# Adding three parts by accumulation on TensorE and one key subtraction on GpSimd, in the adjacency stage of a graph network

## The reference, cut to what matters

```
def _gcn_conv(x, src, dst, W, b, num_nodes):
    h = x @ W
    loops = jnp.arange(num_nodes, dtype=src.dtype)
    s = jnp.concatenate([src, loops])
    d = jnp.concatenate([dst, loops])
    deg = jax.ops.segment_sum(jnp.ones_like(d, dtype=h.dtype), d, num_segments=num_nodes)
    dinv = jnp.where(deg > 0, jax.lax.rsqrt(deg), 0.0)
    norm = dinv[s] * dinv[d]
    msg = h[s] * norm[:, None]
    out = jax.ops.segment_sum(msg, d, num_segments=num_nodes)
    return out + b
```

## Time and profile before

| | us |
|---|---|
| median of 3 runs | 10569.1 (10568.56 to 10575.79) |
| the profiled execution, its own time | 10570.14 |
| its span, first to last instruction | 10568.4 |
| outside the span in that execution | 1.7 |
| first pass, steady part looked at | 2262 to 2885 |
| second pass, steady part looked at | 2960 to 3250 |

### The profile page before, as it was taken

The page is one execution under the profiler, slowest core; times in us unless marked ns, Lnnn a source line. Parts: engine busy times, 40 slices in busy tenths (PEclk is TensorE's granted clock), DMA queues, the critical chain, the costliest instruction groups (busy, mean ns, idle before and its releaser), DMA issues.

```text
span 10568.4 us, 124127 instructions
## 1 busy us (share of the span) xinstructions
PE 5527.7 (52%) x33901; PEld 4454.6 (42%) x33999; DVE 6613.1 (63%) x9196; ACT 2250.9 (21%) x3204; POOL 7100.7 (67%) x7048
## 2 busy tenths in 40 slices
PE   4666656459886666666644423333333434333333
PEld 3444444348885555445522213333333333333333
DVE  6777777789913555555578855555555555555555
ACT  1111111148700111111158821111111111111111
POOL 6777777626604777777755537777777577777774
PEclk8777787679997888888855555556556655556566
DMA  8777777524486777777756625555555355555552
GB/s 182 195 196 194 196 197 197 149 91 206 194 341 219 233 236 237 240 233 234 238 185 203 203 64 125 124 125 124 126 124 126 74 126 124 126 123 126 125 126 67
DMA packets 2347310, 1784.10 MB, mean 169 GB/s; under 512 B 1805829, under 2 KB 1977610, under 8 KB 2342282
## 3 DMA queue, kind: packets, MB, share of 16 engines
q1 hardware_dynamic: 774743, 879.12, 25.3%
q10 hardware_dynamic: 1356944, 617.91, 21.4%
q0 software_dynamic: 215456, 284.72, 11.7%
HBM read 921.34 MB, written 861.11 MB: 169 GB/s over the span
## 4 chain that ended last, share of the span: by engine, by line
POOL 53%; issue 22%; DVE 12%; PE 5%; ACT 4%; DMA 2%; ACTq 1%; SPq 1%; POOLq 0%; DVEq 0%
POOL arena L601 52%; DVE obuf L1894 3%; ACT arena L1116 2%; POOL feat L693 2%; PE ph L927 2%; PE pn L927 1%; DVE neg L1894 1%; DVE pos L1894 1%; ACT obuf L1086 1%; DMA arena<-in_x_dram,idx_src 1%; ACTq L1089 1%; ACT arena L1122 1%; DVE work L1437 0%; DVE arena L1476 0%; PE pn L763 0%
## 5 line engine op out<-in xcount | busy, mean ns | idle before, releaser
L601 POOL DMA_INDIRECT arena<-table_d,idx_src x3136 | 2959.0, 944 | 1123.4 <-issue 955.4
L765 PE MATMUL pn<-work,wblk 128*128 128x128 f32 x3136 | 1049.9, 438 | 2386.3 <-DMA arena<-table_d,idx_src 2386.3
L765 PEld LDWEIGHTS pn<-work,wblk 128*128 128x128 f32 x3136 | 838.0, 327 | 2525.6 <-issue 1844.9
L601 POOL DMA_INDIRECT arena<-in_x_dram,idx_src x1568 | 1495.7, 954 | 514.5 <-issue 469.4
L601 POOL DMA_INDIRECT arena<-tsrc_d,idx_src x1568 | 1479.5, 944 | 477.9 <-issue 477.9
L1378 DVE TENSOR_SCALAR idx_src<-src_all 128x8 int32 (+1 forms) x784 | 147.9, 190 | 2317.9 <-PE pn L766 1590.1
L766 PE MATMUL pn<-ident,arena 128*128 128x128 f32 x4704 | 1375.3, 392 | 0.0
L766 PEld LDWEIGHTS pn<-ident,arena 128*128 128x128 f32 x4704 | 1177.1, 306 | 0.0
L1476 DVE STREAM_TRANSPOSE arena<-work 128x512 f32<-128x512 f32 x1568 | 991.4, 680 | 98.2 <-DVE work L1437 98.2
L1437 DVE TENSOR_TENSOR_SCAN work<-keep,work,pn 128x512 f32<-128x512 bf16 x588 | 752.8, 1280 | 245.4 <-PE ph L778 200.9
L755 PE MATMUL pn<-work,weT 128*128 128x512 f32 x784 | 552.0, 794 | 663.3 <-DMA arena<-tsrc_d,idx_src 634.0
(11 more groups left out here) (402 smaller groups left out, 11166.3 us busy)
## 6 DMA issues: line engine op xcount, KB each, us to landing
runs_d<-arena ACTq DMA_DIRECT2D x2352, 192.0 KB
adj_d<-feat SPq DMA_DIRECT2D x37, 3136.0 KB, 10.8
seed_d<-nothing SPq DMA_DIRECT2D x392, 256.0 KB
arena<-seed_d SPq DMA_DIRECT2D x392, 256.0 KB, 6.8
attr<-in_edge_attr_dram SPq DMA_DIRECT2D x392, 256.0 KB
feat<-total_d SPq DMA_DIRECT2D x196, 512.0 KB
keep<-keep_d SPq DMA_DIRECT2D x588, 128.0 KB
feat<-adj_d SPq DMA_DIRECT2D x37, 1600.0 KB, 9.0
```

What stands on the lines that cost most here:

```text
L601: g.indirect_dma_start(out=to, out_offset=None, in_=table, in_offset=bass.IndirectOffsetOnAxis(ap=idx, axis=0))\
L765: mm(to, wblk[:, PNA.index(p), j, :], feat_to[u], start=True, stop=False, skip_group_check=True)
```

## The change

Two things move. `sum_parts` goes: `local_sum` on PE now multiplies the selection with each of the three parts in turn, reading `vraw` where `vsum` was, and lets the three products accumulate in PSUM. `sums_out` on ACT, which refills `vraw`, therefore waits for PE's product and not for DVE's addition. And `keys` moves from DVE to POOL: it stands there behind the gather of the next step and ahead of the scatter.

```
-                mm(pe_[:, 1, 0:P], pick[:, m % 4, :], vsum[:, m, :], start=True, stop=True,
-                   skip_group_check=True).then_inc(s_used, 1)
+                for k in range(3):
+                    last = mm(pe_[:, 1, 0:P], pick[:, m % 4, :], vraw[:, m % 2, :, k, :], start=(k == 0), stop=(k == 2),
+                              skip_group_check=True)
+                last.then_inc(s_used, 1)
...
-                pe.wait_ge(s_vs, 2 * (MT * x + m + 1))
+                pe.wait_ge(s_vc, MT * x + m + 1)
...
-                    act.wait_ge(s_vs, 2 * (n - 1))
+                    act.wait_ge(s_used, 2 + (MT + 1) * x + m - 1)
...
+                    if m:
+                        keys(m - 1)
                     if m >= ROWS_LAG:
                         local_rows(0, m - ROWS_LAG)
+                keys(MT - 1)
+
+            def keys(m):
+
+                if m == 0:
+                    g.wait_ge(s_kl, 4)
+                g.wait_ge(s_near[m % 2], 16 * (m // 2 + 1))
+                g.sem_inc(s_in_order, 1)
+                g.tensor_scalar(near[:, m % 2, :, 0], near[:, m % 2, :, 0], key0[:, m:m + 1], None, ALU.add).then_inc(s_key, 1)
...
-            def keys(m):
-
-                dve.wait_ge(s_near[m % 2], 16 * (m // 2 + 1))
-                TS(near[:, m % 2, :, 0], near[:, m % 2, :, 0], key0[:, m:m + 1], None, ALU.add).then_inc(s_key, 1)
...
-            def sum_parts(x, m, k):
-
-                n, to = MT * x + m, vsum[:, m, :].rearrange("p (j c) -> p j c", j=2)
-                if k == 0:
-                    dve.wait_ge(s_vc, n + 1)
-                    TT(to, vraw[:, m % 2, :, 0, :], vraw[:, m % 2, :, 1, :], ALU.add).then_inc(s_vs, 1)
-                else:
-                    dve.wait_ge(s_vs, 2 * n + 1)
-                    TT(to, to, vraw[:, m % 2, :, 2, :], ALU.add).then_inc(s_vs, 1)
...
-                            if n == 2 and m + 1 < MT:
-                                keys(m + 1)
-                            if n in (4, 5) and m >= 2:
-                                sum_parts(0, m - 2, n - 4)
```

More of the change, by code:

```diff
@@ L174, in gnn_kernel @@
         key_w = [a[:, :, :].rearrange("p s n -> p (s n)")[:, 0:HOT * KC].rearrange("p (n c) -> p n c", c=KC) for a in (neg, pos)]
-        vsum = work[:, 0:MT * 2 * F].rearrange("p (m n) -> p m n", m=MT)
         rest = work[:, 0:NT * F].rearrange("p (w c) -> p w c", c=F)
@@ L279, in gnn_kernel @@
             "s_tb", "s_td", "s_tail", "s_mi", "s_mid", "s_sc"))
-        s_nat, s_kl, s_key, s_nT, s_nC, s_hts, s_bd, s_ev, s_ap, s_vc, s_vs = (sem(n) for n in (
-            "s_nat", "s_kl", "s_key", "s_nT", "s_nC", "s_hts", "s_bd", "s_ev", "s_ap", "s_vc", "s_vs"))
+        s_nat, s_kl, s_key, s_nT, s_nC, s_hts, s_bd, s_ev, s_ap, s_vc = (sem(n) for n in (
+            "s_nat", "s_kl", "s_key", "s_nT", "s_nC", "s_hts", "s_bd", "s_ev", "s_ap", "s_vc"))
         s_pick, s_used, s_cc, s_ag = (sem(n) for n in ("s_pick", "s_used", "s_cc", "s_ag"))
@@ L1952, in neighbour_sums @@
                     split_table()
-                    keys(0)
                     run_tables()
@@ L1965, in neighbour_sums @@
                     for m in (MT - 2, MT - 1):
-                        sum_parts(0, m, 0)
-                        sum_parts(0, m, 1)
                         pick_run(0, m)
@@ L1971, in neighbour_sums @@
                     for m in range(MT):
-                        sum_parts(1, m, 0)
-                        sum_parts(1, m, 1)
                         pick_run(1, m)
```

## The result

| | us |
|---|---|
| median of 6 runs after | 10649.72 (10646.02 to 10670.37) |
| median of 6 runs before | 10569.65 (10568.56 to 10577.38) |
| ratio | 1.0078 (1.0065 to 1.0090) |
| profiled execution after, its own time | 10670.37 |

A forecast was written before the change was run, and what follows sets the result against it. DVE was taken to bound the first pass, PE the second. 0.2 - 21.2 + 5.4 + 0.8 + 17.0 + 0.9 = +3.1 us on 10570.14, median 1.0 lower: 10572.2, range 10560 to 10588 (own case 10563 to 10581).

The forecast's parts named there:

- The keys on POOL: First pass: keys on POOL stretch DVE's two-input operations by 0.15 us each, 36 x 0.15 = 5.4 us (0 to 10.4).
- -21.2: First pass: 106 small operations (36 keys, 70 additions) leave DVE at 0.20 us each, 21.2 us less.
- 0.8: End of the first pass: two or three selection products stand on the path, 0.8 us more (0 to 1.5).
- POOL becomes the pace: Rival, first pass: keys of 7.3 us on POOL, deciding from 4.2 us; 54 us more, 10626; chance 0.10.
- DVE's distances: First pass: each removed DVE operation counts its distance to the next start, 0.20 us; a round falls from 16.96 to 16.36.
- the burst on PE that just fits: First pass, behind group 1: added products cost 0 (at most 1.8 us); rival that PE takes over: 10582, chance 0.09.
- the second pass: Second pass: two added PE products for each of 34 selections, 0.25 us each, 17.0 us; 0.9 at the very end.
- the rival by which it costs nothing: Rival, second pass: DMA sets the pace and PE only seems full, so added products are free; 10554, chance 0.04.
- the start of the pass: Start of the first pass: hand-over of the first keys to POOL, 0.2 us (0 to 0.5).
- 21 us can't be told from none: Whole kernel: a change under 0.2% (21 us) can't be told from none by a measurement.

The follow-up runs named there:

- experiment 2: Kernel before with only the keys moved to POOL, the additions staying on DVE: ratio 1.0054 (1.0041 to 1.0068).
- experiment 4: Kernel of experiment 3 with the keys on ACT, behind group 5 of each round: 1.0000 (0.9991 to 1.0009) of the kernel before.
- experiment 5: Changed kernel with two more one-input DVE operations a round, behind pairs 0 and 3, results unused: 1.0053 (1.0036 to 1.0070) of the kernel before.
- experiment 6: Kernel before with one more one-input DVE operation a round, behind pair 0, result unused: ratio 1.0007 (0.9998 to 1.0017).
- experiment 3: Kernel before with the parts accumulated on PE in the first pass alone, keys on DVE; run twice: 0.9985 and 0.9986 of the kernel before.
- experiment 1: Changed kernel with the keys left on DVE, so only the additions move to PE, in both passes: 1.0004 (0.9995 to 1.0013) of the kernel before.
- experiment 7: Kernel before, unchanged, run once more for a second trace: 10600.24 us in a single run.
- experiment 8: Kernel before with one key-like operation on POOL ahead of the first pass: 1.0028 (1.0016 to 1.0039).
- experiment 9: Kernel before with 37 key-like operations on POOL in a burst ahead of the first pass: 10611 us in a single run.
- experiment 10: Kernel before with three more semaphore increments on POOL behind each gather of the first pass, 111 in all: 10595 us in a single run.
- experiment 11: Kernel of experiment 3 with one more one-input DVE operation a round, behind pair 4, result unused: 0.9993 (0.9984 to 1.0002) of the kernel before.

## Why the prediction was wrong

Two steps failed. The first is in "The keys on POOL": "The keys are needed by a transposition a round after the gather ahead of them, so that even 3 us behind are hidden", with the 0.15 us of meeting as its whole price. A key waits up to 13.95 us, not 3, and the 5.4 us became a hold that sets the pace: +9.7 us in the first pass where I had -21.2 + 5.4 + 0.8 = -15.0. That is 25 of the 78 us between forecast and result.

The reason is a reading of the earlier trace rows. I took 8.02 us for a scatter as slowness and the 2.248 us of line 610 as the worst that POOL suffers. In the third layer DVE's scans, which read one of their inputs from PSUM, come after at most three contending operations. The 2.248 us ended 0.56 us behind the start of such a scan, so it was the length of that chain, not a bound. The rows held the answer: the ends of gather and scatter lie 0.9 to 1.0 us behind the starts of the selection and the key operation, the only one-input ones in DVE's round. The gather of the earlier trace rows ends at 2630.37, and the selection before that is this:

```profile
2629.45 0.27 DVE L1940 TENSOR_SCALAR arena<-dlo 128x128 f32<-128x128 f32 x1
```

Moving the keys took one of these two places away and added a third customer for them. Experiments 2, 4, 5 and 6 show from four sides that the wait goes by the openings. One SBUF input is not the whole condition, though: line 1448 of the earlier trace rows has one input, of 128x1024, and was stretched to 1.106 us beside POOL.

The rival "POOL becomes the pace" had the right mechanism and the wrong threshold and price. It decided from 4.2 us, which was passed by far, but the wait is not like the scatter's 7.3: it lasts until DVE runs dry, and then everything on POOL passes at once. That is why 54 us were too many for the first pass, where +25 over the forecast were measured. That its 10626 lies nearer to the result than my forecast is luck: it has twice the price in the first pass and nothing in the other layers. (Its sum, 10573 + 54, is 10627.)

The Trainium skill (SBUF — State Buffer, "Who interferes with whom") says that of DVE and GpSimd the one that issues first holds the shared port pair for its whole instruction and that the other fully blocks. By the trace that understates it: key operations wait through a dozen one-hots, 13.94 us. That looks as if the next operation of DVE's queue were first each time, which no run shows by itself. The same section of the Trainium skill has it that a probe did not show `tensor_tensor` stalling POOL's transfers; scatters of 8.02, 3.97 and 16.10 us, by where the one-input operation stands, say that here it does. Two things I can't explain. Transfers also pass beside two-input operations at times: a gather of 1.49 and a scatter of 1.75 us just after DVE has paused, and in experiment 5 scatters of 1.74 and gathers of 1.27 us without any pause. And openings are missed, by the keys of experiment 5 and in the rare long holds.

The second step, and the larger one, is a term that is not in the sum: I put the other layers at nothing without a reason. 52 of the 80 us are there, where the change edits nothing, by gathers that go from 947 to 958 ns. No rival of mine spoke of it. What in POOL makes them slower is open.

Right were: DVE's distances (16.36 us a round when nothing is held, and 16.56 with the additions alone gone), the burst on PE that just fits (DVE waits 0.5 us once in the second trace of experiment 3, so that rival falls), the second pass (+15.5 for 17.0 and the ends; the added product was 0.225 us, between my bounds of 0.22 and 0.26, and the rival by which it costs nothing falls), and the start of the pass (0, within 0 to 0.5). The statement that 21 us can't be told from none was too wide: experiment 3 tells 14 us from none, twice.

Open are the rare holds of 28 to 42 us. In five traces (experiments 1, 6, 7, 8 and the first of 3) they come 188 to 215 us apart, in five (the first of before, the second of 3, experiments 9 to 11) they are missing. Openings are there all the while, and the held operations miss up to five of them.

## What to carry to other kernels

Before an operation or a gather goes to GpSimd beside a full VectorE, list which of VectorE's operations have only one SBUF input. In this kernel the small ones, of 128x128, are where GpSimd mostly gets through, and where they were fewer than its calls its operations were held for 14 to 16 us. Having as many as there are calls (experiment 5) removed nearly all of VectorE's idle time, but not every hold. An engine that is full in one pass and idle in the next asks for a different placement in each: the accumulation on TensorE pays in the first pass and costs in the second. And the length of a waiting operation is to be read by its end, against the other engines' starts, before it is used as a price.

## What the hardware showed that I had not expected

- 37 float32 operations on GpSimd made each of 4704 later gathers longer: 944 to 955 ns (947 to 958 in the changed kernel's trace) among keys held by VectorE, 944 to 952 in a burst.
- Beside a VectorE full of two-input operations, a GpSimd operation of 0.7 us waited 13.94 us, and 14.35 with a short two-input addition among the one-hots, and got through within 0.5 us of VectorE's going idle or of an opening's start.
- The gathers have levels that differ from execution to execution, 944, 947 or 952 ns in the first layer, some 5 to 13 us between the levels for each loop of 1568.
- Three accumulated float32 products of 128x128 take 0.70 us on TensorE, one takes 0.25.
